# Loading x by halves, and leaving late transfers of a projection stage to the attention that follows

## The reference

```
x = L0_attn_x
xn = _layernorm(x, axis=-1)
s = _L0_attn_ref(xn, ...)     # differential attention: 16 heads of 2 maps, 4 key heads, rope,
                              # a1 - lam * a2, causal, norm over all heads, then Wo
g = _silu(_L0_ffn_ref(xn, L0_ffn_weight, L0_ffn_bias))   # both sides rounded to 4-bit blocks of 32
x = x + s * g
xn = _layernorm(x, axis=-1)
s = _L1_attn_ref(xn, ...)     # plain causal attention, 16 heads of 16
g = _silu(_L1_ffn_ref(xn, ...))   # 16 experts, 4 taken per token, and a shared one
x = x + s * g
```

## Time and profile before

| | |
|---|---|
| median of three runs | 869.86 us (868.55 to 869.92) |
| the profiled execution | 868.93 us |
| its span in the trace | 867.2 us |
| PE, DVE, ACT, POOL busy | 88, 61, 50, 50% of the span |
| mean granted TensorE clock | 0.92 of full |

### The profile page before, as it was taken

The page is one execution under the profiler, slowest core; times in us unless marked ns, Lnnn a source line. Parts: engine busy times, 40 slices in busy tenths (PEclk is TensorE's granted clock), DMA queues, the critical chain, the costliest instruction groups (busy, mean ns, idle before and its releaser), DMA issues. The chain is left out here.

```text
span 867.2 us, 12855 instructions
## 1 busy us (share of the span) xinstructions
PE 762.9 (88%) x3632; PEld 365.0 (42%) x3632; DVE 529.4 (61%) x1441; ACT 432.3 (50%) x922; POOL 430.6 (50%) x751
## 2 busy tenths in 40 slices
PE   3938999999999999965984889999669999999995
PEld 2322222222222223222651222322148888888884
DVE  3649787778777768223653867886035555555555
ACT  1431666666666556732141256666534555455552
POOL 1751566654244324321222123334276999799994
PEclk9985999999999999975996698999969999999997
DMA  5393630110020011012059552432221212122221
GB/s 182 130 299 87 154 87 15 43 43 14 20 63 15 21 40 38 21 44 60 1 179 261 129 141 66 126 98 69 87 87 43 66 60 67 52 62 71 62 64 55
DMA packets 60075, 69.83 MB, mean 81 GB/s; under 512 B 14904, under 2 KB 40857, under 8 KB 60010
## 3 DMA queue, kind: packets, MB, share of 16 engines
q1 hardware_dynamic: 60016, 69.15, 28.4%
HBM read 47.35 MB, written 15.47 MB: 72 GB/s over the span
## 5 line engine op out<-in xcount | busy, mean ns | idle before, releaser
L675 ACT ACTIVATE top<-ps 128x512 f32<-128x512 f32 (+3 forms) x384 | 171.0, 490 | 132.4 <-PE ps L622 132.2
L605 PE MATMUL ps<-mid 96*128 96x512 bf16 (+3 forms) x576 | 191.2, 356 | 29.0 <-PEq L981 11.8
L709 DVE CUSTOM_DVE_ANT_0 ps<-ps,keep 128x512 f32<-128x512 f32 (+3 forms) x384 | 184.2, 504 | 41.9 <-PE ps L605 41.2
L622 PE MATMUL ps<-mid 99*128 99x512 bf16 (+3 forms) x576 | 185.7, 338 | 9.2 <-ACT mid L675 6.3
L1450 PE MATMUL ps<-xp,wp 128*128 128x512 f32 (+1 forms) x600 | 149.6, 400 | 14.3 <-ACT wp L1502 8.8
L642 PE MATMUL ps<-top,mid 128*33 128x512 f32 (+3 forms) x768 | 161.6, 500 | 0.0
L622 PEld LDWEIGHTS ps<-mid 99*128 99x128 bf16 x576 | 54.3, 99 | 185.8 <-ACT top L675 103.0
L1450 PEld LDWEIGHTS ps<-xp,wp 128*128 128x128 f32 (+1 forms) x600 | 115.0, 192 | 40.3 <-ACT xp L1504 9.3
L791 POOL TENSOR_SCALAR_AFFINE_SELECT top<-top 128x128 f32<-128x128 f32 x256 | 71.5, 294 | 109.4 <-ACT top L675 107.0
L675 ACT ACTIVATE mid<-ps 128x512 f32<-128x512 f32 (+1 forms) x192 | 82.6, 492 | 69.9 <-PE ps L622 41.8
L713 DVE TENSOR_REDUCE top<-ps 128x1 f32<-128x512 f32 x128 | 88.4, 691 | 36.0 <-PE ps L605 35.5
(11 more groups left out here) (199 smaller groups left out, 777.7 us busy)
## 6 DMA issues: line engine op xcount, KB each, us to landing
mid<-part_scratch SPq DMA_DIRECT2D x9, 1152.0 KB, 8.6
part_scratch<-top SPq DMA_DIRECT2D x18, 384.0 KB, 5.1
top<-in_w SPq DMA_DIRECT2D x16, 396.0 KB, 4.0
cw_s<-combine_rows SPq DMA_DIRECT2D x48, 128.0 KB, 3.0
part_scratch<-top SPq DMA_DIRECT2D x18, 256.0 KB, 5.2
mid<-part_scratch SPq DMA_DIRECT2D x9, 384.0 KB, 3.9
top<-inverse_scratch SPq DMA_DIRECT2D x12, 256.0 KB
top<-in_w SPq DMA_DIRECT2D x8, 384.0 KB, 5.4
```

Source lines behind the costliest of these rows:

```text
L605: nc.tensor.matmul(ps[:, s_bank(turn), 0:w], queries(pair, m)[0:PARTS, i * P:(i + 1) * P], keys(pair, m)[0:PARTS, c * 512:c * 512 + w], st ...
L622: nc.tensor.matmul(ps[:, ST_BANK + n % AHEAD, 0:w], keys(pair, m)[0:STACK, j * P:(j + 1) * P], queries(pair, m)[0:STACK, q0:q0 + w], start ...
L675: nc.scalar.activation(pr[:, n % RING, 0:w], ps[:, ST_BANK + n % AHEAD, 0:w], ACT.Exp, scale=0.25).then_inc(p_ready, 1)
L709: ins = nc.vector.tensor_tensor_reduce(bank, bank, msk[:, 512 - w:512], -1.0 if low else 1.0, 3e38 if low else -3e38, ALU.add, ALU.min if ...
```

## The change

Four things are changed.

- **x by halves.** x is loaded in four transfers of two tiles, with the identity after the second, on a semaphore each. Statistics, inverse roots and normalisation run in halves of four tiles. DVE waits for the identity alone at its start; the mask and the lambdas are loaded later, and DVE handles them inside the loop of units, after the two products of unit 4. The order of the weights is changed; `ws`, `wo_s` and the two norm vectors are no longer loaded here.
- **Late units.** The order of units starts with (4, 0), (0, 0), (4, 1), (0, 1). SP sends these four (`SENT`) and the near gathers of keys and queries 0 in the projection stage. The far gathers of 4 and 0, the parts of the other six units and then the loads of `ws`, `wo_s` and the norm vectors are issued by SP at the start of attention 0 (`early0`). DVE waits for all of them once, at block 1 of the first pair, since the attention's own tiles may then be written over the parts (`sent0`). In the middle the same is done with the last four units and the far gathers (`early1`).
- **Gathers of whole groups.** Groups 1, 2 and 3 of layer 0 are gathered whole, at the turns of pairs 1, 4 and 8. In layer 1 groups 3 and 1 are gathered whole, both in the turn of pair 1, and the first slice of expert weights moves from the turn of pair 0 to that of pair 1.
- **First rows.** The maxima rows of pair 0 are issued by ACT, ahead of its exponentials, on a semaphore of their own.

```diff
-        UN = [(f, c) for f in (4, 0, 1, 2, 3) for c in range(NC)]
+        UN = [(4, 0), (0, 0), (4, 1), (0, 1)] + [(f, c) for f in (1, 2, 3) for c in range(NC)]
+        SENT = 4
...
+            gathered(sp, stack0, at0(f), scr, f, 2, 8, stk0[0])
+
+        def all_maps0(sp, f):
+
+            wait_written(sp, 0, f)
+            gathered(sp, stack0, at0(f), scr, f, 0, 8, stk0[f])
...
+            def written0(sp, u):
+
+                f, c = UN[u]
+                written(sp, scr, f, c, spl[:, u % SLOTS, :, :], f == 4, scr_ok[u % SLOTS])
...
-                    sp.dma_start(xs[:, :, :], x.rearrange("(t p) d -> p t d", p=P)).then_inc(ld_x, 16)
-                    sp.dma_start(idf[:, :], ident).then_inc(ld_c, 16)
-                    sp.dma_start(swp[:, :], swap).then_inc(ld_c, 16)
+                    for n in range(4):
+                        sp.dma_start(xs[:, 2 * n:2 * n + 2, :],
+                                     x[2 * n * P:2 * (n + 1) * P, :].rearrange("(t p) d -> p t d", p=P)).then_inc(ld_x[n], 16)
+                        if n == 1:
+                            sp.dma_start(idf[:, :], ident).then_inc(ld_i, 16)
+                    for t, w in ((wk_s, wk), (wq_s, wq)):
+                        sp.dma_start(t[:, :, :], w.rearrange("(c p) n -> p c n", p=P)).then_inc(ld_w, 16)
+                    sp.dma_start(swp[:, :], swap).then_inc(ld_w, 16)
+                    sp.dma_start(rp[:, :, :], rope.rearrange("m p t -> p m t")).then_inc(ld_r, 16)
                     sp.dma_start(tri[:, :], late).then_inc(ld_c, 16)
...
-                    sp.dma_start(rp[:, :, :], rope.rearrange("m p t -> p m t")).then_inc(ld_r, 16)
-                    sp.dma_start(ws[:, :, :], fw.rearrange("(c p) n -> p c n", p=P)).then_inc(ld_f, 16)
+                    sp.dma_start(wv_s[:, :, :], wv.rearrange("(c p) n -> p c n", p=P)).then_inc(ld_c, 16)
                     for n in range(4):
-                        sp.dma_start(lm[:, n, :], lams[n].partition_broadcast(P)).then_inc(ld_r, 16)
-                    sp.dma_start(wo_s[:, :, :], wo.rearrange("(c p) n -> p c n", p=P)).then_inc(ld_f, 16)
-                    for n, w in ((0, gnw), (1, gnb)):
-                        sp.dma_start(gnc[:, n, :], w.rearrange("(f p) -> p f", p=P),
-                                     allow_slow_non_contiguous=True).then_inc(ld_f, 16)
...
-                    for u, (f, c) in enumerate(UN):
+                    for u in range(SENT):
                         sp.wait_ge(lo_ok, u + 1)
-                        written(sp, scr, f, c, spl[:, u % SLOTS, :, :], f == 4, scr_ok[u % SLOTS])
-                        if u == 2:
-                            near_maps0(sp, 4)
-                        if u == 3:
-                            near_maps0(sp, 0)
-                            far_maps0(sp, 0)
-                    sp.wait_ge(ld_f, 16 * 4)
+                        written0(sp, u)
+                    near_maps0(sp, 4)
+                    near_maps0(sp, 0)
...
-                    link(nc.gpsimd.tensor_scalar(ve[:, :], mv[:, :, 1], EPS, None, ALU.add))
-                    nc.gpsimd.tensor_tensor(rst[:, :], ve[:, :], mhalf[:, :], ALU.pow).then_inc(rstd, 1)
+                    for c in range(NC):
+                        four = slice(4 * c, 4 * c + 4)
+                        pool.wait_ge(stats, 4 * c + 4)
+                        link(nc.gpsimd.tensor_scalar(ve[:, four], mv[:, four, 1], EPS, None, ALU.add))
+                        nc.gpsimd.tensor_tensor(rst[:, four], ve[:, four], mhalf[:, four], ALU.pow).then_inc(rstd, 1)
                     for u in range(len(UN) + 2):
                         if u < len(UN):
                             pool.wait_ge(roped, u + 1)
...
-                    dve.wait_ge(ld_c, 48)
+                    dve.wait_ge(ld_i, 16)
...
+                    for c in range(NC):
+                        for t in range(4 * c, 4 * c + 4):
+                            if t % 2 == 0:
+                                dve.wait_ge(ld_x[t // 2], 16)
+                            last = nc.vector.bn_stats(st6[:, t, :], xs[:, t, :])
+                        link(last)
+                        for t in range(4 * c, 4 * c + 4):
+                            nc.vector.bn_aggr(mv[:, t, :], st6[:, t, :]).then_inc(stats, 1)
+                    dve.wait_ge(stats, NT)
...
+                        if t % 4 == 0:
+                            dve.wait_ge(rstd, t // 4 + 1)
...
+                        if u == 4:
+                            dve.wait_ge(ld_c, 96)
+                            nc.vector.tensor_copy(msk[:, 384:512], tri[:, :])
+                            for n in range(2):
+                                last = nc.vector.tensor_tensor(lp[:, n, :], lm[:, 2 * n, :], lm[:, 2 * n + 1, :], ALU.mult)
+                            link(last)
+                            nc.vector.tensor_reduce(ls[:, :], lp[:, :, :], AX.X, ALU.add).then_inc(lsum, 1)
...
+
+                def rows(eng, pair):
+
+                    eng.wait_ge(s_maxed, maxima_turn(pair) + 1)
+                    for j in range(3):
+                        eng.dma_start(stack[PARTS + j:PARTS + j + 1, 2 * pair:2 * pair + 2, :].rearrange("o m t -> o (m t)"),
+                                      mrow[16 * j:16 * j + 16, :]).then_inc(landed if pair > 0 else landed_first, 16)
+
+                def wait_rows(eng, pair):
+
+                    eng.wait_ge(*((landed, 48 * pair) if pair > 0 else (landed_first, 48)))
...
+                        rows(act, 0)
...
+                            if first and n == 1:
+                                sent(dve)
...
-                            rows(pair)
+                            rows(sp, pair)
                             late(sp, pair)
                             if not first:
+                                if pair == 1:
+                                    weights(0)
                                 weights(pair)
-                        ahead(0)
+                        early(sp)
...
-                pe.wait_ge(near0[4], 16)
-            if pair == 4:
-                pe.wait_ge(stk0[4], 16)
-            if pair % 4 == 0:
-                pe.wait_ge(near0[pair // 4], 16)
-            if pair % 4 == 1:
+                pe.wait_ge(near0, 32)
+            if pair == 1:
+                pe.wait_ge(stk0[0], 32)
+            if pair > 0 and pair % 4 == 0:
                 pe.wait_ge(stk0[pair // 4], 16)
...
+        def early0(sp):
+            far_maps0(sp, 4)
+            far_maps0(sp, 0)
+            for u in range(SENT, len(UN)):
+                written0(sp, u)
+            sp.dma_start(ws[:, :, :], fw.rearrange("(c p) n -> p c n", p=P)).then_inc(ld_f, 16)
+            sp.dma_start(wo_s[:, :, :], wo.rearrange("(c p) n -> p c n", p=P)).then_inc(ld_f, 16)
+            for n, w in ((0, gnw), (1, gnb)):
+                sp.dma_start(gnc[:, n, :], w.rearrange("(f p) -> p f", p=P), allow_slow_non_contiguous=True).then_inc(ld_f, 16)
+            sp.wait_ge(ld_f, 64)
+
         def late0(sp, pair):
-            if pair == 0:
-                far_maps0(sp, 4)
-            if pair < 3:
-                near_maps0(sp, pair + 1)
-                far_maps0(sp, pair + 1)
+            if pair in (1, 4, 8):
+                all_maps0(sp, (1, 4, 8).index(pair) + 1)
+
+        def sent0(dve):
+            dve.wait_ge(ld_f, 64)
+            for u in range(len(UN)):
+                dve.wait_ge(*unit_written(0, u))
...
-            if pair == 4:
-                pe.wait_ge(unit_near, 16 + 5 * 16)
-            if pair % 4 == 1:
-                pe.wait_ge(stk1[2 + pair // 4], 16)
-                pe.wait_ge(stk1[pair // 4], 16)
+            if pair in (1, 4):
+                pe.wait_ge(stk1[pair // 4], 32)
+
+        def early1(sp):
+            far_maps1(sp, 2)
+            far_maps1(sp, 0)
+            for u, parts in left:
+                f, c = UN1[u]
+                written(sp, scr1, f, c, parts, f >= 2, scr_ok[u % SLOTS])
+            sp.wait_ge(comb_kept, 16)
...
-            if pair == 0:
-                sp.wait_ge(comb_kept, 16)
-            if pair < 2:
-                near_maps1(sp, (3, 1)[pair])
-                far_maps1(sp, (3, 1)[pair])
+            if pair == 1:
+                for f in (3, 1):
+                    all_maps1(sp, f)
+
...
+        for u in range(EARLY, len(UN)):
+            env["left"].append((u, spl[:, u % SPL, :, :]))
...
-                for u, (f, c) in enumerate(UN):
+                for u, (f, c) in enumerate(UN[0:EARLY]):
                     sp.wait_ge(lo_ok, u + 1)
                     written(sp, scr1, f, c, spl[:, u % SPL, :, :], f >= 2, scr_ok[u % SLOTS])
-                    if u == EARLY - 1:
-                        near_maps1(sp, 2)
-                        near_maps1(sp, 0)
-                        far_maps1(sp, 2)
-                        far_maps1(sp, 0)
+                near_maps1(sp, 2)
+                near_maps1(sp, 0)
```

70 lines of the change are left out of this document (27 added, 43 removed).

## The result

Before: 868.55 us in the median of 8 runs on the same chip; changed: 873.73 us in the median of 8. The ratio of the two is 1.0064 with a 95% interval of 1.0045 to 1.0082: the change makes the kernel 0.64% slower, some 5.6 us. The ratio leaves out one slow run of the changed kernel (925.93 us, at a mean granted clock of 0.80 instead of 0.91 to 0.92), which the median still contains. I had forecast 869.5 us, just under the 869.86 that the kernel before had on record then. The time lies in the range of 864 to 874.5, but the sign is wrong. The profiled execution of the changed kernel took 874.59 us, of which its span is 872.9.

A forecast was written before the change was run, and what follows sets the result against it. TensorE was taken as busiest, with the gains at seams held open by SP's issuing. From the profiled 868.93 us, -3.1 (layer 0 with opening) and +3.5 (layer 1) gave 869.3; set against the median, forecast 869.5, range 864 to 874.5.

The forecast's parts named there:

- Opening: Loading x by halves starts PE at 10.6 instead of 14.71 us: gain 4.1, net 3.7 after 0.4 lost in DVE's loop.
- The upper bound of 4.5: Upper end of the opening's net gain (1.8 to 4.5 us), described as earlier waking and halves with nothing lost.
- First seam: Attention 0 starts 10.4 us early, DVE waits until 81 us; layer 0 nets 3.1 us won.
- the 2.4 in the sum: Layer 0's loss from PE's low clock after the new stall: 7 us low against 1.8, half lost, 2.4 us (0 to 4).
- Gathers of the second and third map at pairs 4 and 8: Layer 0: 7 us of traffic before outputs DVE's inverse wants, slack about as long; 0 to 1 us each, taken as 0.
- Layer 1 loses 3.5 us: Net of layer 1: outputs behind extra gather and slice land at 520.6 against 517.1; bounds 6 lost to 1.5 won.
- the copy at 520.6: ACT's copy of layer 1's first outputs in pair 1, which land at 494.7 + 15.7 + 10.2 = 520.6 us.
- The bound "1.5 won": Layer 1's favourable bound: 1.5 us won if the gathers run at 245 GB/s and nothing delays the rows.
- the rows' term: First pair's rows on ACT's queue under SP's late writes: 1 us lost (0 to 4), hidden in layer 0, counted in layer 1.
- C: Rival, chance 0.20: rows from ACT's queue wait for SP's late writes, layer 1's scores start 3 us later; 872.5 to 874.
- B: Rival, chance 0.22: PE's clock gains from shorter gaps at both seams, 5.4 us faster than 869.3, giving 864 us.
- D: Rival, chance 0.05: stage release waits for SP's transfers, not its issuing; layer 0 loses about 3, layer 1 about 9: 881.

The follow-up runs named there:

- e10: e9 with the halves of the opening undone (VectorE waits for all of x, GpSimd for all statistics): 857.35 us, against 855.06 for e9.
- e13: e8 with the halves of the opening undone too, leaving the first seam alone: 869.05 us, ratio 1.0005 to the kernel before.
- e8: The changed kernel with middle stage and layer 1 as before, except near and far maps of a group gathered in one transfer: 866.28 us, ratio 0.9974.
- e11: e9 with layer 1's first maxima rows on SP's queue, between far gathers and late units, instead of ScalarE's: 852.43 us, ratio 0.9817.
- e2: The changed kernel with layer 1's two late groups gathered at pairs 1 and 2, one each, instead of both at pair 1: 868.36 us, ratio 0.9998.
- e5: The changed kernel, layer 0's gathers at pairs 1, 6, 10, layer 1's at 1 and 2, weight slices two each at pairs 3 to 5: 863.21 us, ratio 0.9931.
- e9: e5 with one slice at pair 4, later slices respread, and weights, output weights and norm vectors loaded in the first stage: 855.06 us, ratio 0.9839.
- e17: e11 with layer 0's quantising and VectorE's wait one pair later, and layer 0's first rows also on SP's queue before the late units: 850.47 us, ratio 0.9786.
- e14: e8 with all units, gathers and late loads issued within the first stage again, leaving the opening's halves: 871.17 us, ratio 1.0020.
- e16: e9 with layer 1's first rows kept on ScalarE's queue, but SP's late units held until these rows have landed: 852.12 us, ratio 0.9807.
- e12: e9 with layer 0's late gathers at pairs 4 and 8 again instead of 6 and 10: 856.15 us, ratio 0.9848.
- e7: The changed kernel with weights, output weights and norm vectors loaded in the first stage again, behind the lambdas: 869.59 us, ratio 1.0001.

## Why the prediction was wrong

**Opening**: right. PE's first work came 4.0 us sooner (4.1 forecast), 3.1 were left at the end of the first stage (3.7), and 2.3 at the end of the kernel by e10. The upper bound of 4.5 has no working: with nothing lost the sum gives 4.1.

**First seam**: the mechanism was right. VectorE left its wait within 0.2 us of the forecast, though it stood there 3.5 us and not 6: TensorE's waits for the far gathers (3.48 us, which I had not counted in this layer) and for the late rows (1.76, which I had taken as hidden) had already held it up by 2.8. The low clock after the stall lasted to 89 us, 7.9 us after VectorE's release, where I took 7; (7 - 1.8) / 2 is 2.6 and not the 2.4 in the sum. e13 shows the seam, with its gathers, to be worth nothing by itself. Layer 0 with the opening wins 2.3 us (0.7 to 3.8) where I had 3.1, which is no contradiction. One step in it was wrong all the same: "Gathers of the second and third map at pairs 4 and 8" (it is the groups 2 and 3) were "taken as 0", and they cost 1.9 to 2.4 us in the traces. I had the right place (the outputs that VectorE's inverse wants) and saw slack "about as long" as the traffic; slack that is only just covered is a cost, not nothing. What made up for it in the medians is not shown.

**The step that failed is "Layer 1 loses 3.5 us".** With the middle it loses 7.8 (e8), and the terms were too small. Pair 0 lost 4.75 us (35.63 from start to rows of pair 1, against 30.88) where I had 1.8. Its rows were issued 16.33 us after the start instead of 14.15: 2.2 us for the far gathers, for which I had 0.8. Pair 1's rows came 19.30 us after them instead of 16.73: 2.6 us, of which the landing, 4.3 instead of 1.8, gives 2.5, and for which I had 1. (e11 gives 2.6 in the medians for the same thing and 1.9 by the ratios.) The line of the kernel before that answers to the ACTq line above:

```profile
484.66 1.83 SPq L833 DMA_DIRECT2D mid<-mid  x3
```

From pair 1's rows to the outputs' landing it was 27.8 us, not 25.9. A gather costs 8.5 (e2) instead of 7.0, a slice 2.4 instead of 3.2; the remaining 1.2 us are not put down to a term. So the copy at 520.6 became one at 526.4, 0.9 of it from the later start. The bound "1.5 won" on the other side does not follow from its conditions either: without the 1.8 us, and with 6.4 instead of 7.0 us for each of the two gathers, 0.5 are still lost.

The Trainium skill (DMA: Bandwidth & Descriptors, Queues, rings and completion order) says that a DMA engine takes turns between queues, packet by packet. From that I had concluded that the rows' term would be near zero, and I leaned toward it in taking 1 of the 4 us. The trace does not agree with the conclusion: 4.3 us beside SP's writes, 1.8 without them. It does not refute the taking of turns, which no run here shows; turns between queues do not say how soon a transfer beside bulk writes is reported as landed.

**Rivals.** C (rows late behind SP's writes, 872.5 to 874) named both the landing time from which it decides (3 us; measured 4.3) and the result, 873.73. It had 0.20. I argued against it from the median of all landings, though most of those were sent beside light traffic (15 to 17 GB/s in the kernel before over 130 to 160, 200 to 240 and 260 to 300 us) and not beside the 347 to 382 of the late units. C alone does not explain the loss: it gives 1.6 (2.6 instead of 1) of the 4.3 us by which layer 1 was worse than forecast, so that its time came out in part by luck. B (clock gains) did not happen: though the gaps were as short as it says (4.18 and 2.96 us), the clock fell at both seams, and was low for some 34 us from 55 on. D was wrong: attention started at 53.7 and 462.9.

**In sum**: terms of -3.1 and +3.5 cancelled, so the sign hung on errors of 1 us in each; measured, they are -2.3 and +7.8. The sum itself was 0.4 us slower than the profiled run that it starts from. It became a forecast of faster only because it was set against the median, 0.9 higher. All the errors in layer 1 but that of the slice lay on the same side. Most were of transfers that share one set of DMA engines, each priced as if the others kept to time.

## What to carry to other kernels

A stage that is held open by its last transfers can be released early, but the transfers must then find turns with room: what counts is not the bytes in a layer but what stands in the queue ahead of the first output whose buffer is wanted again. Price each turn as (rows to deadline) less (traffic at its measured rate), and move a gather or a slice to a turn without an output that someone waits for: by this alone the same change went from 0.6% slower to 0.7% faster (e5). With four loads taken out from behind the late units and the slices placed better it was 1.6% faster (e9), and 2.1% with the first rows ahead of the late units and the quantising one pair later (e17). Send small urgent transfers before bulk ones begin, whichever queue they use.

## What was not expected of the hardware

- Three transfers of 4 KB on ScalarE's queue landed 3.7 to 4.9 us after issue while SP's queue wrote beside them (382 GB/s over 66 to 78 us and 347 over 478 to 484 in the changed kernel), and 1.7 to 1.8 without, from either queue (e11, e14, e16, e17).
- TensorE's clock can fall after one stall and not after another of much the same length: at pair 4 TensorE was busy 2.53 of the 4 us before it fell (160 to 164, changed kernel), and 2.86 of 4 (156 to 160, e12) where it stayed at 1.00. The fall made that pair up to 1.9 us longer.
- TensorE's granted clock stayed at 0.50 for some 34 us of attention 0's start, with PE busy for 2.4 to 4 of every 4 us but for 64 to 68 and 72 to 76. Without the gap at 80 to 84 it was back 7 us sooner (e7): the stall cost 1.8 us by itself, and about 2 more, by subtraction, through the clock.
